# Attention and a mixture of experts in one kernel: the experts' first twelve tiles from a list made inside attention

## What is computed

```python
x = x + cross_attention(layernorm(x), ctx, ctx)     # 16 heads of 32, 512 keys for each batch
flat = layernorm(x).reshape(4096, 512)
logits = flat @ router_weight.T + router_bias       # 8 experts
scores = softmax(logits)
topk_vals, topk_idx = top_k(scores, 2)              # w[token, expert] = score of the two best, else 0
gu = flat @ gate_up_proj[e] + gate_up_bias[e]       # 512 x 1024 for each expert
gate = minimum(gu[:512], 7); up = clip(gu[512:], -7, 7)
act = (up + 1) * gate * sigmoid(1.702 * gate)
x = x + sum over e of w[:, e] * (act @ down_proj[e] + down_bias[e])
```

## Time and profile before

| | |
|---|---|
| median of 3 runs | 1726.36 us (1724.65 to 1728.31) |
| profiled execution | 1732.28 us, span of its trace 1730.5 us |
| PE busy | 1597.8 us, 92% of the span |
| PE weight loads | 1168.4 us, 68%, beside the matmuls |
| DVE busy | 1272.5 us, 74% |
| ACT busy | 658.1 us, 38% |
| POOL busy | 837.5 us, 48% |
| granted TensorE clock | 0.97 of full, mean |

### The profile page before, as it was taken

The page is one execution under the profiler, slowest core; times in us unless marked ns, Lnnn a source line. Parts: engine busy times, 40 slices in busy tenths (PEclk is TensorE's granted clock), DMA queues, the critical chain, the costliest instruction groups (busy, mean ns, idle before and its releaser), DMA issues. The chain is left out here.

```text
span 1730.5 us, 30244 instructions
## 1 busy us (share of the span) xinstructions
PE 1597.8 (92%) x9612; PEld 1168.4 (68%) x9612; DVE 1272.5 (74%) x2414; ACT 658.1 (38%) x1267; POOL 837.5 (48%) x634
## 2 busy tenths in 40 slices
PE   6889999999899999999998469999999999999995
PEld 4445555555555555555553259999999998999994
DVE  5575777878668778687685668778888778777873
ACT  3354544535445445354444133223323234222320
POOL 3364656566566676566678321423333333423232
PEclk9999999999999999999999769999999999999997
DMA  6342333443434433424331161324543253324321
GB/s 221 84 121 66 106 112 85 112 104 88 121 80 111 103 94 94 116 75 110 92 99 33 56 223 50 101 85 166 172 147 123 87 204 121 107 85 149 116 86 61
DMA packets 101125, 188.99 MB, mean 109 GB/s; under 512 B 28192, under 2 KB 29600, under 8 KB 100960
## 3 DMA queue, kind: packets, MB, share of 16 engines
q1 hardware_dynamic: 79936, 124.25, 25.4%
q0 software_dynamic: 20832, 62.49, 11.4%
q10 hardware_dynamic: 192, 0.26, 0.0%
HBM read 204.32 MB, written 37.51 MB: 140 GB/s over the span
## 5 line engine op out<-in xcount | busy, mean ns | idle before, releaser
L802 DVE TENSOR_REDUCE negmax<-max_ps 128x2 f32<-128x1024 f32 x252 | 307.4, 1220 | 175.5 <-PE max_ps L542 174.1
L671 ACT ACTIVATE pt<-work 128x512 f32<-128x512 f32 x512 | 278.6, 595 | 263.5 <-PE work L554 256.7
L983 POOL TENSOR_TENSOR acc<-acc,pt 128x1024 f32<-128x1024 f32 x128 | 303.8, 2377 | 134.1 <-ACT pt L671 134.1
L1486 PE MATMUL gu_ps<-xgT_hi,wg_hi 128*128 128x256 f32 x1248 | 349.3, 280 | 2.3 <-DVE xgT_lo L1601 1.5
L1486 PE MATMUL gu_ps<-xgT_lo,wg_hi 128*128 128x256 f32 x1248 | 345.8, 277 | 0.0
L1486 PE MATMUL gu_ps<-xgT_hi,wg_lo 128*128 128x256 f32 x1248 | 345.5, 277 | 0.0
L980 POOL TENSOR_TENSOR acc<-pt 128x1024 f32<-128x1024 f32 x64 | 153.3, 2396 | 200.2 <-PE work L574 132.0
L1486 PEld LDWEIGHTS gu_ps<-xgT_hi,wg_hi 128*128 128x128 f32 x1248 | 235.2, 188 | 3.0 <-issue 1.9
L1747 POOL DMA_INDIRECT out<-acc,token_of x78 | 77.2, 989 | 330.4 <-DVE acc L1645 324.6
L1486 PEld LDWEIGHTS gu_ps<-xgT_lo,wg_hi 128*128 128x128 f32 x1248 | 235.5, 189 | 0.1
L1486 PEld LDWEIGHTS gu_ps<-xgT_hi,wg_lo 128*128 128x128 f32 x1248 | 235.2, 188 | 0.0
(11 more groups left out here) (221 smaller groups left out, 2902.2 us busy)
## 6 DMA issues: line engine op xcount, KB each, us to landing
raw_g<-w_gate_up SPq DMA_DIRECT2D x39, 2048.0 KB
raw_d<-w_down SPq DMA_DIRECT2D x39, 1024.0 KB
qs<-q_hi SPq DMA_DIRECT2D x252, 64.0 KB
ks<-k_hi SPq DMA_DIRECT2D x252, 64.0 KB
bd<-b_down SPq DMA_DIRECT2D x39, 256.0 KB
x_in<-x SPq DMA_DIRECT2D x36, 256.0 KB, 3.3
ctxT_raw<-ctx_t SPq DMA_DIRECT2D x32, 256.0 KB, 4.1
xln_dram<-x SPq DMA_DIRECT2D x32, 256.0 KB, 2.8
```

What stands on the lines that cost most here:

```text
L671: e.activation(pt[k % 2][:, h, :], in_work("exp", u, k, h)[:, :], ACT.Exp, scale=scale).then_inc(exped.sem, 1)
L802: e.tensor_reduce(negmax[:, u % 2, n:n + 2], pair_of(u, r)[:, :, :], AX.X, ALU.max, negate=True).then_inc(maxed.sem, 1)
L983: e.tensor_tensor(acc[:, heads, :], acc[:, heads, :], pt[k % 2][:, heads, :], ALU.add).then_inc(added.sem, 1)
L1486: ins = e.matmul(gu_ps[n % GU_BANKS][:, part, :], wg[s][pw][:, k, cols], xgT[s][px][:, k, :], start=(k == 0 and m == 0), stop=(k == KD - 1 ...
```

## The change

- The last eight token tiles form one group, which isn't routed in attention at all. The group of the sixth batch stays there.
- Once the first five batches are counted, attention computes how many whole tiles of 256 tokens each expert has by then (`whole_tiles`, `whole_rows`, on VectorE in steps 27 and 28), and takes the first twelve of them as an early list. SyncE reads their tokens from `token_list` with twelve DMAs of 256 single numbers (`whole_tokens`, step 31), VectorE makes row numbers of them (`token_of`, step 32).
- The weights of the first two early tiles are loaded in steps 30 and 31, over attention's weights (`place_early`), and the first gate weights are split in step 31, round 6. GpSimd fetches the rows of the first two tiles in step 32.
- The routing stage is gone. The expert stage runs the twelve early tiles first, then the other 27 from a list of their own; each list is walked in two halves (`place_of`).
- The routing of the last eight token tiles and of the main list runs on VectorE between the parts of the early tiles' turns: generators of small steps, of which `route(now, f)` runs one for each f (`EARLY_STEPS = (3, 7, 8, 9)` are the turns in which TensorE's share of it is put between the second and third part of its gate_up). GpSimd writes the last eight tiles' places into the list in turns 3 and 4 (16 indirect DMAs), SyncE reads it back in turn 5. Tile 12's rows wait for the result.
- There is one raw buffer for down weights instead of two; tile i's load waits for the split of tile i - 1. `down_hi` on ScalarE moves from the turn's begin behind the second sigmoid.
- The exponential of the last eight tiles' softmax (`soften`) runs on ScalarE in turn 3.

The diff, cut to its core:

```diff
+EARLY = 12
+EARLY_STEPS = (3, 7, 8, 9)
...
-    return [(n, batch) for n in range(0, last, batch)] + [(last, batch - 1), (last + batch - 1, batch + 1)]
-
...
+            if s == EARLY_END + 7:
+                at(2, ("whole_count",))
+                at(3, ("whole_tiles",))
+            if s == EARLY_END + 8:
+                at(3, ("whole_rows",))
+            if s == units[-2]:
+                at(4, *[("load_early", part) for part in "gd"])
+            if s == units[-1]:
+                at(1, ("load_early", "g1"), ("whole_tokens",))
+                at(6, *[("split_early", k) for k in range(C)])
+            if s == units[-1] + 1:
+                at(1, ("token_of",))
+                at(2, ("fetch_early", 0), ("fetch_early", 1))
...
-            g = groups[-2]
-            if s == units[-1] + 1:
-                at(1, ("best", g, 0), ("best", g, 1), ("count", g), ("rank", g))
-                at(2, ("place", g), ("soft", g))
-            if s == units[-1] + 2:
-                at(0, *[("list", g, t) for t in range(GROUPS[g][1])])
-                at(1, ("share", g))
...
+            def whole_tiles():
+
+                e.wait_ge(whole_counted, 1)
+                last()
+                e.tensor_copy(count_i, in_work("whole_count")[:, 0:E]).then_inc(whole_taken, 1)
+                e.wait_ge(whole_taken, 1)
+                then(e.tensor_scalar(whole_i, count_i, FTOK.bit_length() - 1, None, ALU.arith_shift_right))
+                last()
+                then(e.tensor_copy(whole[:, 0:E], whole_i))
+                last()
+                then(e.tensor_tensor_scan(whole_end[:, 0:E], early["ones_e"][:, :], whole[:, 0:E], 0.0, ALU.mult, ALU.add))
+                then(e.tensor_scalar(row_step[:, 0:E], whole[:, 0:E], -float(FTOK // P), float(NT), ALU.mult, ALU.add))
+                last()
+                then(e.tensor_tensor(whole_ended[:, :, :], iota[:, 0:K].unsqueeze(2).to_broadcast([P, K, E]),
+                                     whole_end[:, 0:E].unsqueeze(1).to_broadcast([P, K, E]), ALU.is_ge))
+                then(e.tensor_tensor(whole[:, 0:E], whole_end[:, 0:E], whole[:, 0:E], ALU.subtract))
+                last()
+                then(e.tensor_scalar(whole[:, 0:E], whole[:, 0:E], float(K), None, ALU.min))
+                then(e.tensor_scalar(early["of_expert"][:, :], whole_end[:, 0:E], float(K), None, ALU.min))
+                last()
+                then(e.tensor_tensor(early["of_expert"][:, :], early["of_expert"][:, :], whole[:, 0:E], ALU.subtract))
+
+            def whole_rows():
+                last()
+                then(e.tensor_reduce(expert_of[:, :], whole_ended[:, :, :], AX.X, ALU.add))
+                last()
+                for j in range(FTOK // P):
+                    then(e.tensor_tensor(early["hot"][:, :, j, :], iota[:, 0:E].unsqueeze(1).to_broadcast([P, K, E]),
+                                         expert_of[:, :].unsqueeze(2).to_broadcast([P, K, E]), ALU.is_equal))
+                then(e.tensor_copy(early["expert"][0:1, :], expert_of[0:1, :]))
+                then(e.tensor_tensor(expert_new[:, 1:], expert_of[:, 1:], expert_of[:, :-1], ALU.not_equal))
+                then(e.tensor_tensor(whole_ended[:, :, :], whole_ended[:, :, :], row_step[:, 0:E].unsqueeze(1).to_broadcast([P, K, E]), ALU.mult))
+                last()
+                then(e.memset(expert_new[:, 0:1], 1.0))
+                then(e.memset(expert_new[:, in_list(1, K):in_list(1, K) + 1], 1.0))
+                then(e.tensor_reduce(row_of[:, :], whole_ended[:, :, :], AX.X, ALU.add))
+                last()
+                then(e.tensor_copy(early["changed"][0:1, :], expert_new[0:1, :]))
+                then(e.scalar_tensor_tensor(out=row_of[:, :], in0=iota[:, 0:K], scalar=float(FTOK // P), in1=row_of[:, :], op0=ALU.mult, op1=ALU.add))
+                last()
+                e.tensor_copy(early["row"][0:1, :], row_of[0:1, :]).then_inc(rows_made, 1)
...
+                elif kind == "whole_tokens":
+                    e.wait_ge(rows_made, 1)
+                    e.wait_ge(early["listed"], 16 * TOP_K * EARLY_END)
+                    for i in range(K):
+                        row = e.value_load(early["row"][0:1, i:i + 1], min_val=0, max_val=E * NT - FTOK // P)
+                        e.dma_start(token_in[:, i, :], token_list[bass.ds(row, FTOK // P), :].rearrange("r q -> q r"),
+                                    allow_slow_non_contiguous=True).then_inc(tokens_in, 16)
+                elif kind == "load_early":
+                    part, = what
+                    if part == "g":
+                        e.wait_ge(rows_made, 1)
+                        e.wait_ge(projected["k"].sem, projected["k"][units[-1]])
+                        load_early_gate_up(e, 0)
+                    elif part == "d":
+                        e.wait_ge(projected["q"].sem, projected["q"][units[-1]])
+                        load_early_down(e)
+                    else:
+                        e.wait_ge(v_projected.sem, v_projected[units[-1], 1])
+                        load_early_gate_up(e, 1)
...
+def place_of(n_tiles, early, i):
+
+    K = early["tiles"]
+    return in_list(i, K) if i < K else in_list(i - K, n_tiles - K)
...
-                    down_hi(i + 1, changed_flag(e, i + 1))
...
+                if now == RANK_AT:
+                    soften()
...
+                    if f == 1 and now:
+                        down_hi(now, changed_flag(e, now))
...
-                    gate_up(i + 1, range(KF))
+                    gate_up(i + 1, range(KF // 2))
+                    if i + 1 in (RANK_AT, LIST_AT, FIRST_AT, RUN_AT):
+                        e.wait_ge(xgT_lo_made.sem, xgT_lo_made[i + 2, 0])
+                    if i + 1 == RANK_AT:
+                        rank_last()
+                    if i + 1 == LIST_AT:
+                        choose_rows()
+                    if i + 1 == FIRST_AT:
+                        send_first()
+                    if i + 1 == RUN_AT:
+                        count_run()
+                    gate_up(i + 1, range(KF // 2, KF))
...
+            def best_experts(s):
+                e_of = lambda a: a.unsqueeze(2).to_broadcast([P, LEFT, E])
+                t_of = lambda a: a.unsqueeze(1).to_broadcast([P, LEFT, E])
+                source = masked if s else logits
+                last()
+                then(e.tensor_reduce(best[:, s, :], source[:, :, :], AX.X, ALU.max))
+                last()
+                then(e.tensor_tensor(ranks[:, :, :], source[:, :, :], e_of(best[:, s, :]), ALU.is_equal))
+                yield
+                last()
+                then(e.tensor_tensor(ranks[:, :, :], ranks[:, :, :], t_of(expert_less[:, :]), ALU.mult))
+                last()
+                then(e.tensor_reduce(pick[:, :], ranks[:, :, :], AX.X, ALU.min))
...
+            chain = {(0, 0): (best_experts(0), best_experts(1), count_experts()), (RANK_AT, 2): (share(), place_tokens(), main_tiles()),
+                     (LIST_AT, 2): (take_list(),), (FIRST_AT, 2): (take_first(),), (RUN_AT, 2): (take_run(),)}
+            under_way = []
+
+            def route(now, f):
+                under_way.extend(chain.get((now, f), ()))
+                if under_way and next(under_way[0], "end") == "end":
+                    under_way.pop(0)
+                    if under_way:
+                        next(under_way[0])
+
...
+                    route(now, f)
...
+                if i == K:
+                    e.wait_ge(tokens_known, 1)
+                    e.wait_ge(w_stored, 16 * weights_stored)
...
+                if i == RANK_AT:
+                    e.wait_ge(pos_made, 1)
+                if i in (RANK_AT, RANK_AT + 1):
+                    for t in range((i - RANK_AT) * LEFT // 2, (i - RANK_AT + 1) * LEFT // 2):
+                        list_tile(e, token_list, listed, pos, token, LAST[0], t)
...
+            def load_down(i):
+                e.wait_ge(wd_lo_made[(i - 1) % 2], turn(i - 1) * KF)
+                expert, changed = of_tile(i)
+                e.dma_start(raw_d[:, :, :], w_down[bass.ds(expert, 1), :, :].rearrange("a (k p) f -> p (a k) f", p=P), cond=changed).then_inc(raw_d_in, 16)
...
+                if i == RANK_AT:
+                    e.wait_ge(weight_made, 1)
+                    e.dma_start(w_rows[:, LAST[0]:, :], weight[:, :, :]).then_inc(w_stored, 16)
+                if i == RANK_AT + 2:
+                    e.wait_ge(listed, 16 * TOP_K * (NT - early["listed_tiles"]))
+                    e.dma_start(list_rows[:, :, :], token_list.rearrange("(c p) q -> p c q", p=P)).then_inc(rows_in, 16)
```

727 lines of the change are left out of this document (418 added, 309 removed).

## The result

The changed kernel took 1807.7 us (median of 4 runs, 1802.0 to 1811.6), the kernel before 1725.5 us (1724.4 to 1728.3) on the same chip: ratio 1.048, 95% interval 1.046 to 1.051. It is 82 us slower where 5 us less were forecast. The profiled execution of the changed kernel has a span of 1809.8 us against 1730.5.

What follows compares the result with a forecast made beforehand. TensorE was taken to bound attention and the expert tiles, with a hole between them. Hole - 31.7, expert stage + 25.0, end + 1.5 sum to - 5.2 us on the median of 1726.4: 1721 us, range 1709 to 1736.

Steps and rivals of the forecast that it cites:

- What goes: Between attention and expert stage: the hole goes but its last piece, first expert matmul at 985.4, 33.7 us earlier.
- What attention gets: Attention's end: VectorE bursts cost 1 us, 5 MB of weights 1, token loads 0; gain left 31.7 us.
- rival (b): Attention's end: token loads or weights are late; at 3 us a load + 10 us, 1731; chance 0.12.
- The reloads: Expert stage: 14 weight loads for 8, turns 3 to 13 18.9 us over 17.27; whole stage 25.0 us more.
- the halves of VectorE's turn: Expert turns, cut at the second mix's end: 6.3 and 9.1 us plain, up to 8.4 and 10.8 with weight splits.
- The pairs: Expert stage: loads at neighbouring tiles (17, 18) and (24, 25) cost 4.8 us each, 9.6 together.
- The end: Last expert tiles: tile 38's down-weight split comes ahead of tile 37's mix, 0 to 1.7 us, taken as 1.5.
- At nothing: one raw down buffer instead of two: Expert stage: one raw down buffer, 16 list stores on GpSimd, and SyncE's weights store and list fetch cost nothing.
- TensorE's own added matmuls: 0.5: Expert stage: the matmuls that the change adds on TensorE cost 0.5 us in all.
- (a): Loaded expert turns: restarts at the lower clock, seven turns pay 2 us, + 14; 1735; chance 0.20.
- (c): Expert stage: routing fits in VectorE's gaps, 10 us of turns 3 to 10 and the start go; 1711; chance 0.16.
- (d): Attention's end: no difference that shows, GpSimd's drain stays (+ 3); 1724; chance 0.10.

Runs made afterwards that it cites:

- b1_before_one_gate: The kernel before, with each down-weight load on SyncE waiting for the next tile's down split instead of this one's: 1755.7 us, ratio 1.020.
- e2_no_late_list: The kernel of e1_bias_first without GpSimd's 16 list stores in turns 3 to 5, so the last eight token tiles miss the second list: 1722.5 us, ratio 1.001.
- e3_two_loads: The kernel of e2_no_late_list with weights loaded and split for the first two tiles alone, 12 loads left out: 1706.1 us, ratio 0.991.
- e1_bias_first: The changed kernel with each tile's two bias loads issued on SyncE ahead of its down-weight load instead of behind it: 1740.8 us, ratio 1.011.

## Why the prediction was wrong, point by point

**What goes: right.** Measured from the last row maxima's transfer, so that what happens earlier doesn't blur it, the first expert matmul comes after 90.3 to 91.5 us in three profiles of the kernel before and after 59.0 to 63.4 in the eleven of the changed family that were taken first: 30 us less, where the forecast in this measure was 32.7 (33.7 less the 1 for attention's tail). GpSimd's drain ends at 988.9, VectorE's begins at 991.2. The drain reaches beyond the 985 that I had named as a sign of being wrong, but attention's last logits are 10 us later as well; in all profiles of the changed family it ends before them, in the closest by some 0.7 us. That the profiles show 24.0 and not 31.7 is mostly the start: attention's units stand some us apart from profile to profile, with the same attention too (the second unit's maxima are sent at 74.0 us in the kernel before and at 78.0 in b1_before_one_gate, the eighteenth's at 531.0 and 525.9).

**What attention gets: about right.** The two bursts of VectorE cost 1.1 us in one unit (28.1 where it took 27.0; 1 forecast). The tail, from the last row maxima's transfer to the last logits, is 2.5 us longer on the mean of its scattering values (55.0 to 59.4 us against 53.3 to 56.2), where 1 stood. The token loads were cheaper to issue than I had them (20.8 us for the twelve, not 26), but not by an even price. Their line, and under it how long the first nine and the last three took to land:

```profile
L1268 SPq DMA_DIRECT2D consts_i<-token_list x12: 373/375/7208, 938.5 to 959.0; - x12
...
DMA to landing us min/median/max: 2.0/10.3/12.2
...
DMA to landing us min/median/max: 9.1/10.6/12.2
...
DMA to landing us min/median/max: 2.0/2.0/2.1
```
```profile
937.26 0.40 SPq L1175 DMA_DIRECT2D early_raw_g<-w_gate_up  x1
```

Issue takes 0.375 us each, but at the ninth SyncE is held up for 7.2 us. They are out at 959, where I had 958.5, which is luck: they begin 6 us later than I had it and take 5 less. token_of waits for no DMA, and rival (b) didn't decide.
The Trainium skill ("DMA: Bandwidth & Descriptors", Rules for kernel authors) lowers such loads to one descriptor per element and advises to rearrange them. The trace doesn't show that as their price. The nine that took 9.1 us or more stand behind 2 MB of gate weights, issued 1.2 us ahead of the first of them on the same queue; the last three, issued once SyncE came free again, landed in 2.0 us, near the 1.8 of 8 KB of row maxima. By these rows it is the gate bias's case once more, though no run changed their order.

**The reloads: the sum right by luck, the parts not.** 14 loads, as counted: 56 high parts of gate weights, 52 of them in this stage:

```profile
L1421 ACT ACTIVATE early_wg_hi<-early_raw_g x28: 1040/1057/1062, 1144.5 to 1740.6; 128x1024 fp32r<-128x1024 f32 x28
L1421 ACT ACTIVATE wg_hi<-early_raw_g x24: 1040/1058/1062, 996.3 to 1490.6; 128x1024 fp32r<-128x1024 f32 x24
```

With bias and list out of the way (e2_no_late_list) turns 3 to 13 took 18.0, 18.2, 17.8, 22.4, 25.2, 18.3, 17.9, 17.7, 17.8, 18.8 and 17.8, against 18.0, 19.9, 21.3, 20.9, 19.8, 18.4, 17.3, 17.7, 19.3, 19.3 and 17.0: 19.7 us over 17.27 in all, 18.9 forecast. Turns 6 and 7 are longer than forecast, and the halves of VectorE's turn don't hold the reason. These are their windows in e2_no_late_list:

```profile
1090.22:1112.63 22.41, 19.62 (x130) 17.56 (x129) 20.21 (x46) 8.18 (x15) 8.90 (x8) 0.92 0.48 168
1112.63:1137.83 25.20, 21.18 (x134) 19.87 (x133) 21.44 (x45) 11.12 (x20) 8.80 (x9) 0.86 0.53 158
```

The clock is 0.92 and 0.86 and TensorE is busy 19.6 and 21.2 us for the 17.7 of a plain turn, some 5 us in two turns, and in the second it waits 4.0 us for SyncE's list fetch, which I had put at nothing. That fetch too stands behind 1 MB of down weights, issued 0.4 us ahead of it, and takes 8.8 us to land; in e3_two_loads, where no weights are loaded, it takes 3.7. The pairs were over-costed (4.8 each; 1.6 and 2.1 measured over 17.27, in each pair's one long turn; that the down weights' high part no longer stands in the way is my guess), and single loads later on show no cost. The end came out at 6.8 us in e1_bias_first, where 2.4 stood: 5.9 of that is the longer drain that the list stores leave behind, and without them (e2_no_late_list) it is 2.3. What filled the sum up again is the slower plain turn. ScalarE's two table loads took 1.28 us each, with the exponential between them from 1053.20 to 1056.06, and turn 3 its 18.0 us, as in the sum.

**The step that failed** is the sentence that begins "At nothing: one raw down buffer instead of two". It asks whether the down weights come in time, and they nearly do: in e1_bias_first ScalarE waits at most 2.4 us for them. It doesn't ask what stands behind their load on SyncE: two bias loads, which had been issued a turn ahead and now went out with the tile's first use, behind 1 MB. "Late next" was the gate bias. That is 64 us of the 82 by the ratios (1.048 against 1.011 in e1_bias_first), and 35 when put into the kernel before with its fewer loads.

**The second** is in the same sentence: 16 list stores by their 1.0 us of GpSimd's time. GpSimd had that time. What they hold back is the gathers and stores of sums behind them, for 8 to 13 us behind eight in a row, and, spread, the list itself. With the longer last drain, which the sum had nowhere, they cost 18 us. The 9.7 us of drain behind the last stores in the earlier trace rows could have warned me: I read them as a wait at a stage's end and didn't carry them into the turns. That they are a wait for those stores to land is not shown: the last drain is as long as 7.9 us although the list stores have landed hundreds of us before.

**The third** is "TensorE's own added matmuls: 0.5" with "17.27 in the turns without load after 14": these take 17.36 to 17.79, which is 10.5 us over 23 turns in e3_two_loads.

**Rivals.** (a) Slow clock restarts: the clock was 0.88 and 0.82 in the two worst turns and 0.956 over the run, below the 0.970 before, but as a consequence; without the bias wait it is 0.972 in a kernel that is still slower. Its mechanism is there all the same, in two turns instead of seven (some 5 us, above). (c): in e3_two_loads, with all the routing but neither reloads nor list stores, turns 3 to 13 are 4.6 us over before, and 0.46 a turn of slower pace alone makes 5.1 of that. So where no weights are loaded, the routing all but fits in VectorE's gaps; how much of the loaded turns is routing, no run separates. (d): the drain went.

So the kernel without the first two failed steps is e2_no_late_list: 1722.5 us, 0.1% over before, where -0.3% was forecast. No version that I ran beats the kernel before with the whole output.

## What to carry to other kernels

When a load is made to wait longer, the loads behind it in the issuing engine's program wait as long, and then stand behind its bytes: ask for each of them, by name, when it is first read. A few KB that a first instruction needs go ahead of the megabytes; here moving two bias loads ahead of one load was worth some 64 us. And price an element-wise store by what it holds back behind it, not by the 1 us that its engine shows; if it is spread, ask who reads what it completes. When a small load looks dear, look first at what was issued ahead of it.

## What the runs showed that I had not expected

- TensorE can be busy 100% of a turn at full clock and yet take 17.27, 17.36, 17.67 or 17.78 us for the same 128 matmuls. The pace is even within a turn, differs between the two weight buffers, and was not brought back by the shifts tried or by stream length.
- One wait moved by one turn on SyncE cost the kernel before 2.0% (b1_before_one_gate).
- Of two loads issued within 2 us of each other, 4 KB and 1 MB, the order decided over 45 us of the expert stage in 12 loads, nearly 4 us each.
- Of 12 element-wise loads of 1 KB each, nine behind 2 MB on the same queue took 9.1 to 12.2 us to land, and three after them 2.0 us.
- GpSimd's drain at the end of the expert stage is 7.9 us with 16 list stores in the stage and 2.0 without, although the stores were long over.
